# A GRU followed by a ternary feed-forward block on one core: half group sums in the lone steps, three bf16 parts for the token squares, GpSimd on tile 6's low part at the end

## The reference

```python
def cell(h, x):                       # 32 steps, one after the other
    gi = x @ W_ih + b_ih
    gh = h @ W_hh + b_hh
    r = sigmoid(i_r + h_r)
    z = sigmoid(i_z + h_z)
    n = tanh(i_n + r * h_n)
    return (1.0 - z) * n + z * h

def ternary_quant(w, g=64):           # w in bf16, groups of 64
    scale = clip(mean(abs(w_g)), 1e-8)
    return clip(round(w_g / scale), -1, 1) * scale

gate, up = split(states @ ternary_quant(w_gate_up).T)     # 2 x 1024 columns
h = silu(gate) * up
hn = h * rsqrt(mean(h * h) + eps)     # the mean over the 1024 hidden values
out = x + hn @ ternary_quant(w_proj).T
```

## Time and profile before

| | |
|---|---|
| time, median of 3 runs | 355.58 us (354.89 to 356.31) |
| the profiled execution's own time | 355.06 us |
| its span in the profile | 353.2 us |
| PE busy | 343.9 us, 97% |
| DVE, ACT, POOL busy | 65%, 60%, 49% |
| granted TensorE clock | full speed throughout |

### The profile page before, as it was taken

How to read it: one execution, slowest core, us unless ns; L and a number is a source line. 1 busy time by engine, 2 the same in 40 slices (tenths; PEclk the granted TensorE clock), 3 DMA queues, 4 the chain that set the end, 5 groups by cost and what they waited for, 6 DMA issues and landing times.

```text
span 353.2 us, 5445 instructions
## 1 busy us (share of the span) xinstructions
PE 343.9 (97%) x2026; PEld 298.5 (84%) x2031; DVE 230.1 (65%) x438; ACT 212.8 (60%) x408; POOL 172.5 (49%) x144
## 2 busy tenths in 40 slices
PE   7999999999999999999999999999999999999994
PEld 3788887888888888888888889888898888898894
DVE  6788887899666655656648554675656545744655
ACT  4776767876747566456646656366565556645651
POOL 1022121176735447255363447445462556889882
PEclk9999999999999999999999999999999999999999
DMA  6990000017001000220001000010001000010101
GB/s 226 385 416 16 2 1 2 0 45 314 1 2 59 0 3 1 75 105 1 2 0 61 0 2 0 0 62 1 2 0 59 2 0 2 1 59 2 59 2 60
DMA packets 5570, 17.92 MB, mean 51 GB/s; under 512 B 420, under 2 KB 2084, under 8 KB 5032
## 3 DMA queue, kind: packets, MB, share of 16 engines
q1 hardware_dynamic: 5544, 17.58, 13.1%
HBM read 13.38 MB, written 4.19 MB: 50 GB/s over the span
## 4 chain that ended last, share of the span: by engine, by line
PE 81%; DVE 9%; ACT 3%; issue 2%; DMA 2%; SPq 1%; DVEq 0%
PE ps_ffn L819 29%; PE ps_out L854 16%; PE ps_rz L750 6%; PE ps_rz L751 6%; PE ps_rz L755 6%; PE ps_n L750 3%; PE ps_n L751 3%; PE ps_n L755 3%; PE ps_t L812 2%; DMA x_ring<-in_L_ffn_w_gate_up_dram 2%; PE ps_rz L819 2%; PE ps_t L865 2%; DVE zm_n L519 1%; DVE h_nat L522 1%; DVE o_st L602 1%
## 5 line engine op out<-in xcount | busy, mean ns | idle before, releaser
L285 POOL TENSOR_TENSOR hid_lo<-work,hid_hi 128x512 fp32r<-128x512 f32 x62 | 81.2, 1309 | 112.3 <-ACT hid_hi L352 112.3
L819 PE MATMUL ps_ffn<-st_hi,wguT 128*128 128x512 f32 x236 | 93.3, 395 | 0.3 <-DVE work L536 0.3
L819 PE MATMUL ps_ffn<-st_lo,wguT 128*128 128x512 f32 x236 | 92.6, 392 | 0.0
L292 POOL TENSOR_TENSOR sq_sum<-sq_sum,work 128x512 f32<-128x512 f32 x55 | 74.2, 1349 | 0.4 <-ACT work L364 0.4
L536 DVE TENSOR_TENSOR work<-work,ps_ffn 128x512 f32<-128x512 f32 x55 | 37.7, 685 | 32.8 <-ACT work L348 32.0
L819 PEld LDWEIGHTS ps_ffn<-st_hi,wguT 128*128 128x128 f32 x236 | 44.4, 188 | 8.5 <-DVE work L536 1.0
L819 PEld LDWEIGHTS ps_ffn<-st_lo,wguT 128*128 128x128 f32 x236 | 44.4, 188 | 7.4
L546 DVE TENSOR_TENSOR work<-work,ps_ffn 128x512 f32<-128x512 f32 x63 | 43.2, 686 | 8.2 <-PE ps_ffn L819 6.6
L352 ACT CAST hid_hi<-work 128x512 fp32r<-128x512 f32 x63 | 38.8, 616 | 16.1 <-DVE work L546 16.1
L854 PEld LDWEIGHTS ps_out<-wpT,hid_hi 128*128 128x128 f32 x252 | 37.3, 189 | 4.6 <-DVE o_st L563 1.0
L854 PE MATMUL ps_out<-wpT,hid_hi 128*128 128x256 f32 x252 | 40.5, 283 | 0.1
(11 more groups left out here) (166 smaller groups left out, 681.1 us busy)
## 6 DMA issues: line engine op xcount, KB each, us to landing
out_dram<-o_st SPq DMA_DIRECT2D x7, 512.0 KB, 2.6
xT_all<-in_x_dram SPq DMA_DIRECT2D x1, 3072.0 KB, 17.9
x_ring<-in_x_dram SPq DMA_DIRECT2D x1, 3072.0 KB, 11.4
x_ring<-in_L_ffn_w_gate_up_dram SPq DMA_DIRECT2D x4, 512.0 KB, 9.8
x_ring<-in_L_ffn_w_proj_dram SPq DMA_DIRECT2D x2, 512.0 KB, 10.1
x_ring<-in_x_dram SPq DMA_DIRECT2D x1, 1024.0 KB, 5.6
work<-in_L_cond_W_ih_dram SPq DMA_DIRECT2D x2, 384.0 KB, 4.5
work<-in_L_cond_W_hh_dram SPq DMA_DIRECT2D x2, 384.0 KB, 6.1
```

Of the source, the lines that this page charges most:

```text
L285: nc.gpsimd.tensor_tensor(hid_lo[:, j % RING], hid[:, j % 2], f32(hid_hi[:, j % RING]), ALU.subtract).then_inc(hid_lo_ok, 1)
L292: nc.gpsimd.tensor_tensor(sq_sum[:], sq_sum[:], hid_sq[:, j % 2], ALU.add).then_inc(sq_added, 1)
L819: mm = pe.matmul(bank, w, group_state(part, G, k), start=(k == 0 and i == 0), stop=(k == KD - 1 and i == 1))
```

## The change

**In the lone steps.** The two matmuls of `q_group_sums` are issued apart: the first half before the transposes of an odd step, the second after the state product of the next even step (both stood after `input_n` of the odd step). `q_means(u)` moves behind the tanh of the even step, `q_signs(u)` takes its old place, `q_weights(u - 1)` goes to the odd step, and `q_sign` gets two buffers. From step 2 on the n bank of step t+1 is seeded by an ACT copy (`seed_n(t + 2)`, one step earlier) in place of two PE matmuls. GpSimd's `xT_lo` subtraction waits for the r gate as well.

**Token squares of groups 0 to 4.** `sq_sum` is split into three bf16 parts (`limbs`): ACT copies the first and the second, DVE subtracts twice. PE then makes 12 bf16 matmuls of one column in place of four float32 ones. For these groups GpSimd adds tile 7's square before it makes tile 7's low part. In a group's first step the input product `n` and `G1` move ahead of the transposes, so that only `U1` stands behind them, and DVE and ACT work tile 1 in that step.

**The end.** Tile 6's low part goes to GpSimd, the adding of tile 6's square from GpSimd to DVE, the square of half `a` from DVE to ACT, and `T6` (the token squares of `sq_sum`) stands ahead of `Ta`.

```diff
-PE_BEFORE = [["C6", "G0", "in", "C7", "S", "U0"], ["G2", "U2", "in", "D0"],
+PE_BEFORE = [["C6", "G0", "in", "C7", "U0", "G1", "S", "n"], ["G2", "U2", "in", "D0"],
...
-PE_AFTER = [["n", "G1", "U1"], ["n", "G3", "U3", "D1"], ["n", "G5", "U5", "D3"], ["n", "D5"]]
+PE_AFTER = [["U1"], ["n", "G3", "U3", "D1"], ["n", "G5", "U5", "D3"], ["n", "D5"]]
+PE_ONSET = [["G0", "in", "U0"], ["n", "G1", "U1"]]
...
-          "U5", "D3", "G6", "U6", "D4", "Ga", "Ua", "D5", "Gb", "Ub", "Ta", "T6", "Tb", "D6", "Da", "Db"]
+          "U5", "D3", "G6", "U6", "D4", "Ga", "Ua", "D5", "Gb", "Ub", "T6", "Ta", "Tb", "D6", "Da", "Db"]
...
+        def in_limbs(G):
+            return G <= NG - 4
+        limbs = [q[:, 0, :] for q in (q_mean, q_kept, q_scale)]
...
             for t in range(2, LEAD + 2):
                 pool.wait_ge(x_hi, t + 1)
+                pool.wait_ge(r_ok, min(t, LEAD))
...
+                if j == HT - 1 and in_limbs(G):
+                    add_square(G, j)
+                    low_part(G, j)
+                    return
+                low_part(G, j)
+                if j and n < NG * HT - 2:
+                    add_square(G, j)
...
+            def first_limb(G):
+                act.wait_ge(sq_added, 7 * (G + 1))
...
+                nc.scalar.copy(limbs[0], sq_sum[:]).then_inc(limb_1, 1)
+            def second_limb(G):
+                act.wait_ge(rest_1, G + 1)
...
+                nc.scalar.copy(limbs[1], sq_sum[:]).then_inc(limb_2, 1)
...
             for t in range(LEAD):
                 u, odd = divmod(t, 2)
                 r_gate(t)
+                if t == 0:
+                    bias_tile()
+                elif odd and u:
+                    q_weights(u - 1)
+                else:
                     q_signs(u)
...
                 z_gate(t)
                 n_gate(t)
                 if odd:
                     q_abs_of(u + 1)
                 elif u:
-                    q_weights(u - 1)
+                    q_means(u)
...
+                if 0 < t < LEAD - 1:
+                    seed_n(t + 2)
...
                 n_gate(t)
+                if G and s == 0:
+                    first_limb(G - 1)
                 if t < T - 1:
                     seed_n(t + 1)
...
+                if squares:
+                    second_limb(G - 1)
+                    hidden_hi(G, 0)
+                    silu_part(G, 1)
                 state_hi(t)
...
             last_silu("a")
             hidden_square(G, 6)
+            last_hi("a")
             last_silu("b")
-            last_hi("a")
+            act.wait_ge(sq_added, 7 * NG - 2)
+            nc.scalar.activation(hid_sq[:, 1, 0:2 * P], hid[:, 1, 0:2 * P], ACT.Square).then_inc(sq_last, 1)
             last_hi("b")
...
+            def first_rest(G):
+                dve.wait_ge(limb_1, G + 1)
+                nc.vector.tensor_tensor(sq_sum[:], sq_sum[:], limbs[0], ALU.subtract).then_inc(rest_1, 1)
+            def third_limb(G):
...
+                nc.vector.tensor_tensor(limbs[2], sq_sum[:], limbs[1], ALU.subtract).then_inc(limb_3, 1)
...
                 new_state(t)
+                if squares:
+                    first_rest(G - 1)
...
-                if G and s == 0:
+                if squares:
+                    third_limb(G - 1)
+                    hidden(G, 0)
                     mean_square(G - 1)
                 state_lo(t)
...
-                if G and s == 0:
+                if squares:
+                    gated(G, 1)
+                    hidden(G, 1)
                     rows_out(G - 1)
...
-            nc.vector.tensor_tensor(hid_lo[:, j % RING], hid[:, j % 2], f32(hid_hi[:, j % RING]),
-                                    ALU.subtract).then_inc(hid_lo_ok, 1)
             last_gated("a")
             last_hidden("a")
-            last_square("a")
+            dve.wait_ge(sq_added, 7 * NG - 2)
+            dve.wait_ge(hid_sq_ok, HT * NG - 1)
+            nc.vector.tensor_tensor(sq_sum[:], sq_sum[:], hid_sq[:, 0], ALU.add).then_inc(sq_added, 1)
...
                 for s in range(GS):
-                    mm = pe.matmul(ps_sq[:, s:s + 1], sq_sum[:, s * P:(s + 1) * P], ones[:], start=True, stop=True)
+                    for i, part in enumerate(parts):
+                        mm = pe.matmul(ps_sq[:, s:s + 1], part[:, s * P:(s + 1) * P], one,
+                                       start=i == 0, stop=i == len(parts) - 1)
...
             for t in range(LEAD):
                 if t:
                     state_product(t)
+                if t and t % 2 == 0:
+                    q_group_sums(t // 2, (1,))
                 seed_rz(t + 1)
                 input_rz(t + 1)
-                seed_n(t + 1)
+                if t < 2:
+                    seed_n(t + 1)
...
+                if t % 2:
+                    q_group_sums((t + 1) // 2, (0,))
                 transpose_state(t)
                 input_n(t + 1)
-                if t % 2:
-                    q_group_sums((t + 1) // 2)
...
                 state_product(t)
+                if t == LEAD:
+                    q_group_sums(4, (1,))
```

More of the change, by code:

```diff
@@ L98, in gru_ffn @@
         q_abs = sb("q_abs", [P, 2, 2, 512], BF16)
-        q_sign, q_mean, q_scale, q_keep, q_kept, q_signed = (
-            sb(n, [P, 2, 512], BF16) for n in ("q_sign", "q_mean", "q_scale", "q_keep", "q_kept", "q_signed"))
+        q_mean, q_scale, q_keep, q_kept, q_signed = (
+            sb(n, [P, 2, 512], BF16) for n in ("q_mean", "q_scale", "q_keep", "q_kept", "q_signed"))
+        q_sign = sb("q_sign", [P, 2, 2, 512], BF16)
         q_ones = sb("q_ones", [P, P], BF16)
@@ L331, in seed_n @@
             def seed_n(t):
[L332 to L333 removed]
+                act.wait_ge(n_pre_ok, t - 1 if t <= LEAD else t)
+                nc.scalar.copy(n_bank(t), bias[:, 1, :]).then_inc(n_seed, 1)
             def n_gate(t):
@@ L472, in _ @@
                 silu_part(G, 7 if s == 3 else 2 * s)
+                squares = G and s == 0
+                if squares:
+                    second_limb(G - 1)
+                    hidden_hi(G, 0)
+                    silu_part(G, 1)
                 state_hi(t)
@@ L475, in _ @@
                     q_abs_of(5)
-                hidden_parts(G, 2 * s)
-                if s < 3:
+                if squares:
+                    hidden_square(G, 0)
+                else:
+                    hidden_parts(G, 2 * s)
+                if s < 3 and not squares:
                     silu_part(G, 2 * s + 1)
@@ L672, in _ @@
                 last = g == NG - 1
-                if s:
+                squares = G and s == 0
+                if s and not (G and s == 1):
                     if t != LEAD + 1:
@@ L702, in _ @@
                     hidden(G, 7)
-                if s == 0:
+                if s == 0 and not squares:
                     hidden(G, 0)
@@ L860, in token_squares @@
             def token_squares(G):
-                pe.wait_ge(sq_added, 7 * (G + 1))
+                if in_limbs(G):
+                    if not G:
+                        pe.wait_ge(consts, 6)
+                    pe.wait_ge(limb_1, G + 1)
+                    pe.wait_ge(limb_2, G + 1)
+                    pe.wait_ge(limb_3, G + 1)
+                    parts, one = limbs, ones_b[:]
+                else:
+                    pe.wait_ge(sq_added, 7 * (G + 1))
+                    parts, one = [sq_sum[:]], ones[:]
                 if G:
@@ L902, in last_squares @@
                     mm = pe.matmul(ps_sq[:, s:s + 1], squares[:, s * P:(s + 1) * P], ones[:],
-                                   start=(s == 0 and part == "a"), stop=part == "b" or (part == "6" and s < 2),
+                                   start=(s == 0 and part == "6"), stop=part != "6",
                                    skip_group_check=True)
@@ L1007, in _ @@
                 before, after = PE_BEFORE[s], PE_AFTER[s]
+                if t == LEAD:
+                    before, after = PE_ONSET
                 if s == 3 and G == 0:
```

74 lines of the change are left out of this document (42 added, 32 removed).

## The result

The changed kernel takes **352.2 us** (median of 4 runs, 351.43 to 352.8) where the kernel before took 355.94 beside it (4 runs): a ratio of 0.9904, 95% interval 0.9882 to 0.9926. In a later set of runs it took 351.72 against 355.71, 0.9883 (0.9861 to 0.9906). So it is 1.0 to 1.2% faster; forecast were 351.7 us and 0.989.

What follows compares the result with a forecast made beforehand. PE was taken to bound the groups, a chain round all engines the lone steps. Lone part 1.65, token squares 1.75 and end 0.40 made 3.8 off 355.06: 351.3, given as 351.7 us on the median's scale, range 350.3 to 353.7.

Steps and rivals of the forecast that it cites:

- Even lone steps: Steps 2, 4, 6: without two group sums ahead of the state product, 0.47 us saved each, 1.41 in all.
- The second limit: DVE in even lone steps: r_hn right behind q_signed gives 5.37 us, 0.30 saved, if q_signed stays as long.
- Odd steps: Steps 1, 3, 5, 7: half sum needing q_abs ahead of the transposes, 0 taken; bounds 0 and 0.9 us lost.
- Step 8 and its like: Step 8: 0.47 us gained ahead of its state product, a half sum of 0.23 behind it: 0.25 saved.
- Rival 3: Lone steps give nothing: the half sum behind q_abs costs odd steps what even ones gain; 353.3 us, chance 0.09.
- Token squares: Twelve bf16 loads at 0.55 us an item against 0.90 in float32: 0.35 saved five times, 1.75 us.
- rival 2: Token squares: the bf16 items cost 0.25 us, by the difference of the loads; 350.2 us, chance 0.07.
- The rule of the Trainium skill: Token squares: about 81 ns per load with its matmul, so 12 pairs cost 0.97 us and the kernel ends at 353.8.
- Rivals 1 and 5: Token squares: 1, float32's cost through a floor per pair, 353.4 us, chance 0.15; 5, same-column matmuls wait, 360, 0.04.
- The state's way back: Each group's first step: U1 alone covers st_hi with 0.3 us to spare, so the new order costs nothing.
- rival 4: State late in each group's first step, ACT first copying tile 0's high part: 0.3 us five times, 353.2, chance 0.07.
- The end: From 340 us: T6 starts at 345.25 in place of 345.65 after DVE's add of 1.27 us, 0.40 us saved.

Runs made afterwards that it cites:

- e6: The changed kernel without GpSimd's wait on the r gate in the lone steps: 352.95 us, 0.993 of the kernel before.
- e1: The kernel before with the part on the lone steps alone: 354.12 us, 0.9967 of the kernel before.
- e10: The kernel before with two SBUF tiles that nothing uses, no instruction different: 356.14 us in one run.
- e5: The changed kernel with the token squares of all groups in float32 again, the new order kept: 354.0 us, 0.9954 of the kernel before.
- e2: The kernel before with the bf16 token squares of groups 0 to 4 and their new order alone: 353.63 us, 0.9951 of the kernel before.
- e7: The changed kernel with three bf16 matmuls, their results unread, in PE's wait ahead of T6: 351.19 us, 0.9885 of the kernel before.

## Why the prediction was right, step by step

- **Even lone steps: 1.41 us forecast, 1.35 measured** (0.44, 0.47 and 0.44). The z gate comes 0.44 earlier against its transposes, as reckoned. The second limit did not bind, since `q_signed` fell to 0.69; e6 shows that 5.37 us was too dear for the case in which it stays at 1.11.
- **Odd steps: 0 forecast, 0.13 lost in all** (0.03 to 0.04 in each). The half sum needs `q_abs`, which ends at 21.00; the sum starts at 21.05 and the transposes follow at 21.28 without a wait. e6 shows how thin this is: without the wait on GpSimd each odd step loses 0.23 us, the bound that the prediction gave (0.9 in all).
- **Step 8 and its like: 0.25 forecast, 0.40 found** (0.21 in step 8 and 0.19 in steps 9 to 11). The sum of the lone part, 1.65, is met by 1.62 from profile to profile and 1.72 in e1 against the right base. Rival 3, that the lone steps give nothing, fell.
- **Token squares: mis-sized, 0.55 us an item forecast and 0.29 measured.** I stood nearer to the ratio of the load durations (0.70) "since each pair must also be issued"; the difference of the loads (0.25) came nearest. Eight float32 passes 0.112 apart and twelve bf16 pairs 0.025 apart mean that the issue of a pair costs no more than 0.025. The item before was sized too high as well: I took 0.90 us from one weight load to the next, but the first load runs under the matmul ahead of it, and in the chain the eight passes are 0.79. So the item saved 0.50 us, where I had put 0.35 and rival 2 0.65; 0.44 of it reached the period, 0.05 went elsewhere, by e10 most likely to the new addresses, and 0.39 five times is some 1.94 us, against 1.75 forecast.
- **The rule of the Trainium skill** that I set against this part, 81 ns a pair ("TensorE: Matmul & The Clock Gate", section "Back-to-back issue gap"), does not hold for these matmuls: it is stated for 128 columns. The same section has a table with a row for 1 to 64 columns, an issue floor of about 25 ns, stated for a matmul by itself. The trace shows that figure, 0.025 us, for a matmul together with its load. Rivals 1 and 5 fall by the same rows: a pair costs 0.025 us, also where three matmuls add into one PSUM column.
- **The state's way back: right.** `st_hi` ends and the state product starts behind `U1` with no wait of PE, and e5 prices the order at nothing, so rival 4 fell. What comes nearly late instead is the third part itself, 0.2 us once in e2 and in e6.
- **The end: 0.40 us forecast, 0.22 measured up to T.** DVE's add took 1.45 us beside GpSimd's low part where I gave it 1.27, and that is as much as the whole difference (341.72 where the sum put 341.54). In the Trainium skill "SBUF — State Buffer", section "Who interferes with whom", says that a VectorE operation with two SBUF inputs and a GpSimd operation that reads SBUF exclude each other, the second blocking until the first is done. As an estimate by that rule the add would end 0.69, what DVE's subtraction of that shape takes in `first_rest`, behind GpSimd's 341.03, at 341.72. It ends at 341.58, so the trace agrees to 0.14 us.
- **The clock: not in the sum at all.** The sum was made against an execution at full clock, and the 0.5 us that I added up to the median of the runs was most likely the fall in the others. The changed kernel's clock fell in 8 of 9 executions, so it came out nearly even on the scale of medians. Luck has a part in that: where the clock falls, it costs the kernel before 1.2 us and the changed one 0.56, a gain that no term of the sum holds. The same sum makes a span of 349.4 us, and the profiled one is 349.87, for the 0.56 us behind T. (351.3 and 0.5 also make 351.8, not the 351.7 that I wrote.)

Up to T the sum comes out at 3.77 us for the 3.8 forecast over all, by errors that nearly cancel: token squares 0.19 and the steps from 8 on 0.15 better, even steps 0.06, odd steps 0.13 and the end 0.18 worse. The 0.35 us of e10 over the whole, already taken off the squares here, could be seen in no view of before.

## What to carry to other kernels

When one engine waits for a shared one, a wait added to the right instruction can be worth more than work taken away: a `wait_ge` on GpSimd gave 0.9 of the 1.6 us of the lone part, because two operations stopped sharing time with each other. Price an operation that the trace doesn't hold from the difference of its parts as well as from their ratio, and where the bounds are a factor of 3 apart keep the middle. Look at the granted clock of the last microseconds in every execution, not only in the profiled one, before a sum is made against its span; and compare the parts of a change on a base that has the same tiles in memory, with more than one profile of each.

## What the runs showed of the hardware

- A pair of a bf16 load of 128 x 128 and a matmul of one column takes 0.025 us in a row of twelve, in which each three add into one column.
- DVE's bf16 operation of 128 x 1024 takes 0.69 us alone and 1.11 beside GpSimd's subtraction of 128 x 256, and that takes 0.77 to 0.79 alone and 1.26 beside it. Both get longer, so a mean of either hides the sharing.
- The mean granted clock of TensorE was 0.988 to 0.995 in 41 of 55 executions of the kernel before and in 8 of 9 of the changed one; in their profiles (e10, and both of the changed kernel) it was at half in the last microseconds. Ahead of the fall, from 344.4 us on, PE had waited 0.70 us in the changed kernel and then worked through 1.8 us of one-column matmuls; with the wait filled (e7) it stayed full in 4 of 6.
- With two unused tiles in SBUF, 2 KB and 2 bytes in each partition, a group's period, in which PE is never idle, was 40.91 us in place of 40.86 (one profile of each).
